# A two-layer decoder on one core: new written orders for the parts of the five engines

## The reference

```python
x = _layernorm(x + _L0_attn_ref(x, ...))                 # 7-wide windowed attention, 16 heads
x = _layernorm(x + _L0_xattn_ref(x, ctx, ctx, mask, ...))  # attention to the context
x = _layernorm(x + _L0_ffn_ref(x, Wr, Wqkv, Wo))         # 8 experts choose 16 rows each and attend among them
x = _layernorm(x + _L1_attn_ref(x, ..., gamma))          # attention scaled by a decay mask
x = _layernorm(x + _L1_xattn_ref(x, ctx, Wq, Wkv, Wc))   # memory rows chosen by argmax, then 16 heads
x = _layernorm(x + _L1_ffn_ref(x, w1, conv_w, conv_b, w2))  # quantized linear, 3-tap conv, silu, quantized linear
```

## Time and profile before

| | us |
|---|---|
| time, median of 3 runs | 1125.49 (1124.31 to 1127.63) |
| span of the profiled execution | 1122.6 |
| TensorE busy | 969.1 |
| VectorE busy | 943.0 |
| ScalarE busy | 750.2 |
| GpSimd busy | 140.0 |
| DMA queue 1, share of 16 engines | 16.7% |

### The profile page before, as it was taken

One profiled execution on the slowest core, in us unless ns is written; L12 is line 12 of the kernel. 1 busy time (PEld: TensorE's weight loads), 2 busy tenths in 40 slices (PEclk: granted clock), 3 DMA queues, 4 the chain that ended last, 5 costly groups with the idle time before them and its releaser, 6 DMA issues.

```text
span 1122.6 us, 19705 instructions
## 1 busy us (share of the span) xinstructions
PE 969.1 (86%) x7038; PEld 695.0 (62%) x7038; DVE 943.0 (84%) x2503; ACT 750.2 (67%) x1854; POOL 140.0 (12%) x401
## 2 busy tenths in 40 slices
PE   5768879999999999999999999989999888786552
PEld 3545657666767676767676676757576666564331
DVE  4799766689898989899999989898989886868854
ACT  2223454758696878778687868786868786767643
POOL 2000110101111020202020111111020201011000
PEclk8879899999999999999999999999999998999865
DMA  7832023011111212020303020211202000000000
GB/s 205 319 105 75 22 63 94 1 56 30 56 49 38 66 29 75 20 85 10 94 10 94 9 85 11 66 38 39 66 30 66 17 3 20 1 20 1 10 10 10
DMA packets 36626, 58.90 MB, mean 52 GB/s; under 512 B 6784, under 2 KB 15872, under 8 KB 36016
## 3 DMA queue, kind: packets, MB, share of 16 engines
q1 hardware_dynamic: 36528, 57.64, 16.7%
...
## 4 chain that ended last, share of the span: by engine, by line
DVE 52%; PE 31%; ACT 12%; issue 4%; POOL 1%; DMA 0%; SPq 0%; ACTq 0%; DVEq 0%; POOLq 0%
PE bank_c L444 9%; DVE area_f L1248 8%; PE bank_a L444 6%; PE banks_e L444 5%; DVE area_a L990 4%; DVE area_a L1034 4%; DVE neg_top L1181 4%; DVE area_f L1239 3%; DVE x L874 3%; DVE area_a L1038 3%; PE bank_f L444 2%; DVE area_f L1257 2%; PE bank_x L444 2%; ACT squares_out L1322 2%; DVE area_f L1263 2%
## 5 line engine op out<-in xcount | busy, mean ns | idle before, releaser
L1248 DVE SCALAR_TENSOR_TENSOR area_f<-area_f,w_convw 128x254 f32<-128x254 f32 x256 | 111.9, 479 | 10.3 <-ACT area_f L1548 7.8
L1548 ACT ACTIVATE area_f<-area_f,w_convb,w_convw 128x256 f32<-128x256 f32 x128 | 69.8, 594 | 29.1 <-DVE area_f L1239 28.7
L1310 ACT ACTIVATE area_bx<-bank_x 128x512 f32<-128x512 f32 (+1 forms) x144 | 70.0, 498 | 27.1 <-PE bank_x L638 15.6
L990 DVE TENSOR_TENSOR area_a<-area_a 128x512 f32<-128x512 f32 x112 | 73.0, 682 | 14.5 <-ACT area_a L1310 13.7
L1181 DVE TENSOR_REDUCE neg_top<-banks_e 128x8 f32<-128x1024 f32 x64 | 76.1, 1216 | 7.6 <-PE banks_e L444 7.3
L1310 ACT ACTIVATE area_a<-bank_a 128x512 f32<-128x512 f32 (+1 forms) x80 | 44.0, 550 | 49.1 <-PE bank_a L444 33.6
L1310 ACT ACTIVATE area_bx<-bank_c 128x512 f32<-128x512 f32 x64 | 34.5, 539 | 63.0 <-PE bank_c L444 59.9
L1034 DVE TENSOR_TENSOR area_a<-area_a 128x512 f32<-128x512 f32 x112 | 74.3, 684 | 0.4
L1519 ACT ACTIVATE area_e<-banks_e 128x512 f32<-128x512 f32 x128 | 68.6, 594 | 1.4 <-PE banks_e L795 1.4
L1038 DVE TENSOR_TENSOR area_a<-area_a 128x512 f32<-128x512 f32 x96 | 65.7, 684 | 0.3
L444 PE MATMUL bank_x<-area_bx 128*128 128x128 f32 (+1 forms) x256 | 54.8, 348 | 5.7 <-ACT area_bx L1454 4.2
...
## 6 DMA issues: line engine op xcount, KB each, us to landing
...
area_a<-in_xT SPq DMA_DIRECT2D x16, 256.0 KB, 2.9
x<-in_x SPq DMA_DIRECT2D x16, 256.0 KB, 2.8
area_bx<-in_ctxT SPq DMA_DIRECT2D x16, 256.0 KB, 2.7
area_d<-in_ctxT SPq DMA_DIRECT2D x16, 256.0 KB, 2.6
y<-x SPq DMA_DIRECT2D x16, 256.0 KB, 2.2
...
```

Source lines behind the costliest of these rows:

```text
L990: return dve.tensor_tensor(product_of(wi).rearrange("p (n t) -> p n t", t=P), qT0.rearrange("p c (b t) -> p (c b) t", t=P), kT0.rearrange( ...
L1248: last = dve.scalar_tensor_tensor(c4[:, i, :, dst], h4[:, i, :, src], cwt3[:, 2 * jj + i, k:k + 1], c4[:, i, :, dst], ALU.mult, ALU.add)
L1310: return act.activation(dst, src, ACT.Copy)
L1548: last = act.activation(c4[:, i], h4[:, i], ACT.Identity, bias=w["convb"][:, j:j + 1], scale=cwt3[:, j, 1:2])
```

## The change

The strings of `ORDER` are replaced by others; the entry of SyncE also moves to the end of the dictionary, which has no effect. No part, instruction, buffer or wait is changed. The dependences between parts are the same, and so is `BANK_TURNS`. Of VectorE's strings the first three lines stand here, ScalarE's are left out.

```diff
-    "SP": (
-        "SASASAASASBSSCSBSAAABAAABAAACAABACBAACFABAACFABAACFABAACFABAACFABAACFABAACFABAACFABAACFABAACFABACFCFCFFF"
-        "F"
-    ),
     "PE": (
-        "AAAAAASSSSSAABABABABASABABBXXBAAXSAXAXAXABBAXASXBBXXXXXBAAXBXASXAXAXBXABXBXBACXACXCXCXXCCXCAACXCACACXCAE"
-        "XBXEBABEBXBEBACXAECXECECXXECXCXCXEAXCECECACXACFEBAFBEFXBAFXBAXEXFBEBACFAXCEXCEXCXECXCFXCEXECFECEACACFCXA"
-        "EXBFAFEBFXABXFBXAEXFBEBACXAFCEXCEXCXECXCFXCEXECFECEACACFCXAEBFXAFEBFABXFXBXAEXFBEBACAXFCEXCEXCXEXCCFXCEX"
-        "ECFECEACACFCXAEBFXFAEBFXABXFBXAEXFBEBAXCAFCEXCXECXEXCCXFCEXECFECEACAXCFCAEBFXAFEBFXABXFBXAEXFBEBAXFCACEX"
-        "CEXCXEXCCXFCEXECFECEACAXCFCAXEBFAFEBFXABXBXFAEXFBEBAXCFACEXCEXCXEXCCXFCEXECFECEACAXCFCAXEBFAFEBFXBAXFBXA"
-        "EXFBEBAXCFACEXCEXCXEXCCXFCEXECFECEACAXCFCAXEFABFEBFXBAXBFXAEXFBEBAXCFACEXCEXCXEXCCXFCEXECFECEACAXCFCAXEB"
-        "FAFEBXFBAXFBXAEXFBEBAXCAFCEXCEXCXEXCCXFCEXECFCEAECAXCFCAXEBFAFEBFXBAFXBXAEXFBEBAXCAFCEXCEXCXEXCCXFCEXECF"
-        "ECEACAXCFCAXEBFAFEBFBXAFXBXAEXFBEBAXCFACXECEXCXEXCCXFCEXECFECEACAXCFCXEBFEBFBFXBXFXEXFBEBXCFECXECEXCXFXE"
-        "CXCXCXEFECECFCXCCFCFECFECFXCEXFEXFXECEXCXEXCFXEXCFXEXECECFCCCEFCEFCFECFEFECECEFCECECCEFECFCEFEFFFEFEFEFE"
-        "EEEFEFEFFFFFFFFFF"
+        "AAAAAASSSSSAABABABSABABAABXBBXSAAXXAABAXABXAAXBXXXXSBXXAABXXABXABXAXBXSABXBXACAXCXXCXCXCCXCAACXCACXACXCA"
+        "EBXEBBABEXBEBAXCAECEXCXECXXECXCEXECXCACECACCXABFEAXFFBFABEBAXFXEXBBEACXFEACXCXECXEXCCXFEXECCFECEACACFCAE"
+        "XXFBAFEXFABFXBABXEXBFEABAXFCECXCXXECXCECXFECXFCECEACEACFCAXEXFBABFEXFBXABFXEFXAEBBXFACEAXCCEXCXXECXCFECE"
+        "FXCECEACACFXCAEBXAFBXFEXBFXBAFEAXABFBEFXCEACXCECXXECCXEXFCEXCEFCEACACFCXAEFXBAFEXFBAFBXEBXFABXEBAXCAFXCE"
+        "CECXXEXCCXFECFEXCECEACAXCFCAXEBFAXBFEFXFABXBAEFXBBECAFAXCEXECCXEXCXCFXECEXCEFCEACXACFCAEBXFAEFBXFXFABXFB"
+        "EXAFEBBAXCXEACCECXXEXCCFXECEXCFECEXACACFCAEBXAFEBXFFBAFXEBXFABXEFBAXCACEXCCEXXCEXCXFECEXCEFCAECACFCAXEXF"
+        "BFAFEXBXBABFEXAFXBAEBACXFCXECEXCXXECCXCEXFCECFAECEACFCXAXEBFABFEFXAXFBXBFEXBAEFBXAXECACCEXCXXECCXFECEXEC"
+        "FECACAXCFCAEBXAFEBFFXABXFBXFEXBEABFEAXCEAXCCXCXEXCCXFECEXCEFCXEACACFCEBXFBFEFBXFXBXBXEFEBXCEFCXECXEXCFXE"
+        "CXCEXEFCECCFCXCXCEFCFXFCEXFXCEFCEXFECEXCXEFXXCXFEXCEXECECFCCCEFCEFFCEFCEECFECECFECCECEFECFCEFEFFFFEEFFEE"
+        "EEFEEFEFFFFFFFFFF"
     ),
     "DVE": (
-        "SAAAAAAASASSSAAAAAAAAAAAAAASSAAAAAABAASSABBAAAAAAAAAAAAAAXSAXSXAAAAASAAXBAXAAAAAAAAAXAAAAABBXSAXXXAAAAAX"
-        "BBAAXBXAAAAAAAACAAAAAXCACAAXCXCAAAAAXEEEEEABABXBAAXEAAAAACAAXAAAACCAAXEECAFCXEEAAAAEFXEFFEBAXFFABAFFXBFF"
-        "AFFFXAECFFAAFACCAFXAAAAAAEFAFFAAFEXCAFCFEEXAEAEFAXFAXEBFAFFAABFFXBFAFFFFXAECFFAAFACCAXAFAAAAEAAAAFFFFECX"
...
+        "AAAAASAASSASSAAAAAAAAAAAAAASASSAAAAABAASBABAAAAAAAAAAAAASAXAXSAAAAASAAXXABABXAAAAAAAAAXAAABAXSAXXAAAAABB"
+        "XXAABXAAAXAAAAAACAAXCAACAAAXCXCAAAEEAAEEEXBAAXBBAAXEXAAACAAACACAEXAAAAAECACFXEEFAAAAAFFXEEBEXFFFAABXBFFF"
+        "FFAFXAECFFAAAXCFCAAAAAFEAAAAFFAFFECXAFCFEEXAAAXFAEFEFAEBAAFFFBXXBFFFFFAXFAECAFCFAAXFCAAAFAAAAAAEAFFFFCEX"
...
     ),
...
     "POOL": (
-        "ABABXABXCABCXEABCEXAFBCEXAFBCEXAFBCEXAFBCXEAFBCXEAFBCXEAFBCEXAFBCXEAFBCEXAFBCXEAFBCXEFCXEFCEFEFF"
+        "ABAXBABXCABCXEABCEXAFBCEXAFCBEAXFBCEXAFBCXEAFBCXEAFBCXEAFBCEXAFBCXEAFBCEXAFBCXEAFBCXEFCXEFCEFEFF"
+    ),
+    "SP": (
+        "ASSSSAAABSSSBSAAAASAABBCAAACAABACAAACBFAAABCFAAACBFBAAAFBAAACFAAACCBFAAABFBAACAFAACABCFAAABCBFAACFCFFCFF"
+        "F"
     ),
```

More of the change, by code:

```diff
@@ new lines @@
+        "FAECAAAFFCAACXFAAAAAEFAAXAFFFEFCAFCFEEXAAFEAEXEFFBAAFFFBAAXXBFFFAFFFXAECFFCAAAXFCFAAAAAEAAAAFFAFXFCEAFCF"
+        "XEEAAAXFAEEFFEBAFFFBAABXXFFFFFAFXEAXCFFACAAFCAAAAAFEAAAAFXAFFFECAFCFEEXAAAXFEEFFEAFFBFABAAXXFBFFFAFXFAEC"
+        "FFACXAAFCAAAFAAEAAAAXFAFFFECAFCFEEXEEXFAAAEFFBXAFFFAABAXBFFFAFFFXACEFFACXAAFCAAAFAAEAAAAAFXFFFECAFCFEEXA"
+        "AAXFEEAEBFFABAAFFFXXBFFFFFAFXAECFFCAAAXFCAAAAAAAAAFAEXFFFFCEAFCFXEEAAAAXFEEFFEBFFFABXXAABFFFAXFFFAXECAFF"
+        "CAAFCAAAFEAAAAAAFEAFXFFCAFCFEEXEEAAXFAEFFBFFFXAAXABABFFFEAFFXFACFFAAACFXCAAAFAAEXAAAAFFAFFECAFCFEEXFXEEB"
@@ L94 @@
+        "FFEFFFXXBBFFFFFFXEFFFXCFCCEXFFFFEFCFCXEEFXEEFFEFFFCFFFFFXFXFFEXFCXCFFFEFFXECFCFEEEEFEFFCFFFECCFFFFFFFFEF"
+        "CFEFFCFFEEFFEEFEFFFFFFFFEFFFFFFFEFFFFEFFFFFFFFFFFFFFFFFFFFFFF"
     ),
     "ACT": (
-        "AASAASASSSSSABAAABABABSABABBBXBXAAAAXAXAXBAXBABXXXXXBXABBXXBXAAASAXAXBXBXBXABCXABCXCXXCCXCXACCXCAXCAACAC"
-        "AXBXBBEBXBEEEEABCXAEBCXCEEEXECXCXEXCCCXCAEXCXECEAXAACFBAFBFABFXFBXFEFXBFFEEEAECFXFACBFEXCFXBXCEFCXEEECXE"
-        "CCCFECFFFAEXECAXFXCAFAXBFAFBFABXFFXBEFFXBFFEEEAECXFAFCBFEXCFXBXCEFCXEEECXECCCECFFFAFECXEAFCXXAFABFXAFBFA"
@@ L104 @@
[L104 to L107 removed]
+        "AAASASSASSAABAABASBASSBBAABBXBBXAAAAAXABXXAXABBXXXXXXABBXXXABAABAXBAXBXBXAXCAXXCXBCSXBCCXCXAXCCCXACAAACC"
@@ new lines @@
+        "XABBXBBEBXEEEAECXAEBCXBCXEEEXECXECXCCCCXEACXXECEAXCAAFAFBBFABFFXBXFEBXFFEEECEFAFFXFACBXECXBFXCXCFEEEEXCE"
+        "CCCECFFAFFECXEACFXXAAXFFAFBFABBXFFXBEFBXFFAEEEEFCXFFCBEAXXCBFXFCXCFEEEECXCCECCEAFFFFECXEACXXFAXAFBAFBFFB"
+        "AXFFXEFXBBFFEEEEXACFFFCEAFXCBFXXCXFCEEEEXCECCCBECAFFFFEACEXCAAXXBXFAFFFBXBFAXBFFEXBFFFAEEEECFXFFCAXBECBX"
+        "FFCXCEEEEXFCXECCCECFFAXFFECEACXXFAAXFFAFBFBBXAFFBXEBFXFFEEEAEXFCFFCABFFECXBXXCFCXEEEEXCECCCECFFAXFFECXEX"
+        "ACXFAAFBAFFXBFABXFFEBFBFFXEEEACEXFFFCEFBACFXBXCXCFXEEEECEXCCCECFFAXFFEXCEACXFAAXBFFAFFBXABFFXEFBXFFBEEEE"
@@ new lines @@
+        "FXACFFCBAEFCXFXBXCFCXEEEECXECCCECXFFAFFECAEACXAXFBXFAFFBBFXAFFXBEXFBFFEEEAEFCXFFACEBCFFXXCXCBFXEEEECXECC"
+        "CEFACFFFEXECAXCFXAAXFFBFABBFXBAXFFEFABXFFEEEECXFFFCBAECXBXFFXCXCFEEEECXECCCCAEXFFFFXECAEXFCXAFABFAFBFAXB"
+        "FFXBFEXBFFEEEEXBFACEFFACXBFCFXXCXCFEEEECEXCCECFCAFFFEXACEXCXAAFXFBAFFBFBXFFXBEABXEEEEFFFEAXFCFFCAXBCFFXB"
+        "XCFCEEXEECXECCCXECXAFFFFEACXECFFBXAFBFBFXBXFFXFEBFFEEEEXCFEFFCBFFXBXCFXEEEECXCEXCEXCCFCFFFECXEXFCXFCFFCF"
+        "CXXFFCFEFFEEEFEFFFEXCFCXFXEEXCXEEXCCEXCFFFFECXEXCEFCCFFFCFCEFFEEEECFECFFCEEEFECCFFCEFFCFECFCFFFEEFFFFFEF"
```

18 lines of the change are left out of this document (2 added, 16 removed).

## The result

The new orders are slower: 1128.66 us (median) against 1126.27 us, ratio 1.0034 with a 95% interval of 1.0021 to 1.0047. The work is the same, as the busy times show (compare); the chain that ended last has changed sides (compare: 52% VectorE, 31% TensorE).

The account below looks back on a forecast made before the run. The prediction took TensorE and VectorE handing the chain to each other as the bound, with the middle's chain on VectorE. Middle 0, start -5.0 and end -1.8 gave -6.8: 1125.5 to 1118.7 us; own range 1114 to 1122, 8-in-10 range 1108 to 1140.

Parts of the forecast that it names:

- rival R1: Middle: slower, new pairs' waits reach the end, +7.0, 1132.5 us; mark is TensorE idle over 36 us; chance 0.31.
- Step 1: Middle, 240 to 880 us: TensorE waits that go, together -7.4 us.
- (a): Middle, TensorE: nine waits before the memory station's turn `aT` go, -3.3 us.
- (b): Middle, TensorE: waits before decayed's `qk` for ScalarE's copy shrink, -2.0 us, bounds 0 and -4.1.
- (c): Middle, TensorE: waits of cross's `pv` for its copy go, -2.1 us.
- Step 2: Middle, TensorE: 18 more adjacent dependent pairs add 14.4 us of waits, taken to fill slack, 0 on the end.
- the period's mark: Middle: the prediction is wrong if the period leaves 59.7 us by more than 0.5 us.
- Step 3: Start, VectorE: work moved inside three long waits, -5.0 us, bound 0.
- Step 4: End: experts' gather of group 15 stands four parts earlier on TensorE, -1.8 us, bound 0.
- Step 5: SyncE: context loads held up to 44 us behind other loads stay hidden, 0.
- R2: Start and middle: no change, group 0's chain sets the middle's begin and the middle cancels, 1125.5 us; chance 0.25.
- R3: Middle: larger gain, removed waits count and new pairs don't, 1111.3 us; chance 0.12.

Follow-up runs that it names:

- The three kernels with more work: Before's orders, windowed's value turns tripled on TensorE, first product doubled on VectorE, or value copy doubled on ScalarE, groups 4 to 13: 1131.48, 1131.54, 1134.47 against 1126.64 us.
- the version with only pairs: Before, with decayed's score product moved ahead of the experts' turn on TensorE in nine groups: 1132.10 against 1125.66 us, ratio 1.0052.
- The start alone: New orders of all five engines up to about 246 us, before's orders behind: 1125.67 against before's 1125.66 us, ratio 0.9995.
- the end alone: Before's orders up to about 870 us, new ones behind: 1125.48 us, ratio to before 1.0006.
- part of the 3.3 us: Gain over before of new orders up to about 246 us and after about 870 us, old between: 1123.08 against 1126.38 us, ratio 0.9966.
- behind the old start: Before, with new orders only from about 246 to about 870 us: 1135.64 us, ratio to before 1.0097.
- the versions with the pairs apart: TensorE neighbour exchanges separating dependent parts: 21 or 70 on the changed kernel, 1137.37 or 1165.69 us; 34 on before, 1151.57 us.

## Why the prediction was wrong

The forecast was 1118.7 us and faster; the result is slower by 0.34%. It is rival R1 by its mechanism, and not by its time: R1 had 1132.5.

**Step 1, waits that go.** Right in kind, a little large. (a) went in full: the 3.3 us before `aT`. (b) fell from 3.2 to 2.2 us, so -1.0 where -2.0 stood. (c) didn't come: cross's `pv` waits 2.1 us before and 1.9 after, now as pairs. The prediction had counted this part twice, as a wait that goes here and as a new pair in four groups in step 2. Not foreseen: the waits before decayed's `xT` fell from 3.0 to 1.1 us. Together with the rest the idle away from pairs went from 23.1 to 17.9 us, -5.2 for -7.4.

**Step 2, waits that come: the step that failed.** The count held (27 pairs in groups 4 to 12; 29 pair waits in the stretch), the price was too high (0.54 us measured, 0.80 taken), so +10.8 for +14.4. The error was the sentence "I take it that the chain stays on VectorE, so the new TensorE waits fill slack and cancel against part 1". I took idle time for slack: 31 us of idle on TensorE seemed to have room for 21.6 us of waits. The version with only nine more pairs lost 3.2 us in seven periods for 3.3 us of new pair waits. The three kernels with more work show no such room in windowed's chain on TensorE, VectorE or ScalarE, though these idle 4%, 6% and 23% of the seven periods. The idle of before is made of short waits for another engine, each with more work behind it. Most of a new wait at another place doesn't fill them; it comes on top (in the version with only pairs 5.2 us of new waits took 2.4 us of others away). The chain's 52% on VectorE told where the time passes in the trace of before, not what a change would cost. In after it names TensorE with 62%, for the same work.

VectorE's wait of 2.05 us before the feed_forward residual didn't stay, against the prediction. After has, in two periods and in all:

```profile
590.92 0.48 DVE L874 SCALAR_TENSOR_TENSOR x<-bank_f,area_f,x 128x256 f32<-128x256 f32 x1 [1.61 <-PE bank_f L444]
...
651.53 0.48 DVE L874 SCALAR_TENSOR_TENSOR x<-bank_f,area_f,x 128x256 f32<-128x256 f32 x1 [1.61 <-PE bank_f L444]
...
DVE x L874 <- PE bank_f L444: 16.3, 10, 2.0
```

These two lines stand 60.6 us apart (59.7 before): the period's mark, 59.7 by more than 0.5, is crossed. And the 2.9 us that this wait gave back didn't help either, as 3.0 us more came before windowed's residual.

The sum of steps 1 and 2, +10.8 - 5.2 = +5.6, is the added idle of TensorE in 240 to 880. The seven periods lose 7.1, of which 4.9 are idle and 2.2 are longer busy time. That second term stood nowhere in the prediction; what it is made of isn't shown (last section).

**Step 3, the start.** -5.0 was too much. Of the three waits of the earlier trace rows, the 3.89 us before the rotation of group 1 are gone, but cross's score step, which now stands ahead of it, waits 2.06 us itself, and the rotation starts 1.2 us later than before; 2.01 fell to 1.02 before the second half of memory's maxima, and 5.03 to 4.20 before memory's residual. Two other waits grew: before the chosen key (L1166) from 0.78 to 2.19, and before the rotation of group 2 from 0.32 to 1.72. The long wait before windowed's residual stayed (4.45 before, 3.75 now). After, VectorE in order of time, 140 to 222 us:

```profile
140.52 0.42 DVE L1052 SCALAR_TENSOR_TENSOR area_bx<-bank_c,w_xmask 128x256 f32<-128x256 f32 x1 [2.06 <-PE bank_c L444]
...
142.84 0.49 DVE L1110 TENSOR_TENSOR area_bx<-area_bx 128x128 f32<-128x128 f32 x2
...
167.42 0.42 DVE L874 SCALAR_TENSOR_TENSOR x<-bank_a,x 128x256 f32<-128x256 f32 x1 [3.75 <-PE bank_a L444]
...
177.39 0.42 DVE L1166 TENSOR_TENSOR chosen_key<-bank_c,w_parity 128x256 f32<-128x256 f32 x1 [2.19 <-PE bank_c L444]
...
194.28 0.49 DVE L1110 TENSOR_TENSOR area_bx<-area_bx 128x128 f32<-128x128 f32 x2 [1.72 <-ACT area_bx L1310]
...
221.81 0.42 DVE L874 SCALAR_TENSOR_TENSOR x<-banks_e,x 128x256 f32<-128x256 f32 x1 [4.20 <-PE banks_e L444]
```

VectorE's idle up to 240 us fell by 2.2 us in this execution, and the first windowed product of group 5 stands at 236.91 us, 2.0 ahead of before, where about 5 were forecast. The start alone gave 0 in the time; the one gain that repeats in the traces is the 1.1 us in the period from group 5 to group 6. Work that is put into a wait leaves the place where it stood before; if that place was cover for something else, a wait opens there. For these waits this is read from the rows and not tested one by one. The step behind windowed's products cost nothing that can be seen: VectorE begins with five products at 15.44 us, where four began at 14.14, and the first product of windowed group 1 stands at 48.1 us on TensorE, where it stood at 48.7.

**Step 4, the end.** -1.8; the end alone was 0. With the new start it may be part of the 3.3 us.

**Step 5, SyncE.** Right: 0, as the run with the old order of loads shows. No DMA stands before cross's first product.

**The rivals.** R1's mark was the right one: TensorE's idle over 36 us in the middle, and it is 36.5. Its size was not: +7.0 stood for the whole middle, which loses 1.0 us in each period and 10 to 11 us in all behind the old start; that the whole change loses only 2.4 us (medians) to 4 (means) comes from the period around the joint and from the start, whose gain R1 had as eaten. R2, no change, lies outside the interval, and R3 is excluded, as added pair waits count. The Trainium skill (Perfetto Trace Analysis, Optimizing Tensor Performance, Matmuls) says that independent matmul groups should take turns on different PSUM banks, so that one is emptied while the next is filled. The trace agrees that two parts in a row in one bank wait for the copy between them, 0.47 us in the mean in the version with only pairs. But in each of these pairs the second part also reads what the copy makes, so no run here tells the bank from the operand. And the versions with the pairs apart show that what comes between must have its own operand ready.
